# Second cross-attention of a decoder: turned copies behind the exponentials, products ahead of turning

## What is computed

```python
scores = jnp.einsum('bhqd,bhkd->bhqk', qh, kh) / math.sqrt(D_K)
scores = jnp.where(mask == 0, -jnp.inf, scores)
attn = jax.nn.softmax(scores, axis=-1)
attn = jnp.nan_to_num(attn, nan=0.0)
x = jnp.einsum('bhqk,bhkd->bhqd', attn, vh)
```

## Time and profile before

| what | value |
|---|---|
| median of 3 runs | 1338.29 us (1337.8 to 1340.01) |
| span of the profiled execution | 1336.9 us |
| busy PE / DVE / ACT / POOL | 86% / 82% / 62% / 61% |
| second attention, first scores to last scores | 1055.1 to 1261.0 us |
| rows of the profile that the change touches | L1088 to L1097 (DVE), L872 and L882 (ACT), L977 (POOL), L708 and L637 (PE) |

### The profile page before, as it was taken

The page is one execution under the profiler, slowest core; times in us unless marked ns, Lnnn a source line. Parts: engine busy times, 40 slices in busy tenths (PEclk is TensorE's granted clock), DMA queues, the critical chain, the costliest instruction groups (busy, mean ns, idle before and its releaser), DMA issues.

```text
span 1336.9 us, 17670 instructions
## 1 busy us (share of the span) xinstructions
PE 1155.3 (86%) x6026; PEld 672.1 (50%) x6026; DVE 1095.1 (82%) x1618; ACT 828.6 (62%) x1827; POOL 821.0 (61%) x743
## 2 busy tenths in 40 slices
PE   7798888878588999989989899899987888888874
PEld 4555555544244544545545455455454555555544
DVE  3577777575889999999999999999999768776556
ACT  2555555565477677866777668776754365566564
POOL 6001111100698998988989989899899344455405
PEclk9899999988889999999999989999897999999975
DMA  6000002000602305015041060230500300100000
GB/s 203 13 12 13 12 12 71 1 1 5 226 8 94 147 1 198 17 48 193 1 169 45 1 241 1 94 120 1 198 31 0 80 17 17 32 17 2 1 1 25
DMA packets 22142, 79.15 MB, mean 59 GB/s; under 512 B 4935, under 2 KB 8847, under 8 KB 21138
## 3 DMA queue, kind: packets, MB, share of 16 engines
q1 hardware_dynamic: 22054, 78.02, 16.8%
HBM read 76.77 MB, written 1.24 MB: 58 GB/s over the span
## 4 chain that ended last, share of the span: by engine, by line
PE 38%; DVE 33%; POOL 10%; ACT 10%; issue 7%; DMA 0%; SPq 0%; ACTq 0%; DVEq 0%; POOLq 0%
PE ps L637 36%; DVE ps L1954 10%; POOL arena L1868 6%; DVE arena L1959 4%; DVE arena L1957 4%; DVE hstat L1097 4%; ACT arena L872 3%; POOL arena L1880 2%; ACT ps L1751 2%; PE ps L708 2%; DVE arena L1917 2%; ACT L632 1%; ACT arena L882 1%; DVE arena L1085 1%; DVE arena L1063 1%
## 5 line engine op out<-in xcount | busy, mean ns | idle before, releaser
L637 PE MATMUL ps<-arena 128*32 128x100 f32 (+8 forms) x3300 | 521.0, 383 | 81.7 <-ACT arena L872 26.1
L1868 POOL TENSOR_TENSOR arena<-arena 128x1600 f32<-128x1600 f32 x128 | 456.4, 3580 | 35.4 <-DVE ps L1954 27.2
L637 PEld LDWEIGHTS ps<-arena 128*32 128x32 f32 (+6 forms) x3300 | 262.3, 146 | 298.2 <-issue 109.2
L637 PE MATMUL ps<-arena,ident 128*128 128x400 f32 x1024 | 386.2, 528 | 29.3 <-POOL arena L1880 19.6
L1751 ACT ACTIVATE ps<-arena 128x400 f32<-128x400 f32 x512 | 282.9, 590 | 184.5 <-DVE arena L1957 151.3
L1954 DVE TENSOR_TENSOR_SCAN ps<-ps,arena 128x800 f32<-128x800 f32 x176 | 320.6, 1822 | 22.7 <-ACT ps L1751 17.0
L637 PEld LDWEIGHTS ps<-arena,ident 128*128 128x128 f32 x1024 | 201.9, 200 | 197.6 <-issue 29.2
L872 ACT ACTIVATE arena<-ps,hstat 100x361 f32<-100x361 f32 x256 | 143.6, 563 | 107.1 <-DVE hstat L1097 107.0
L610 POOL TENSOR_SCALAR stat<-stat 100x1 f32<-100x1 f32 (+1 forms) x44 | 8.6, 196 | 289.8 <-DVE stat L591 288.6
L1957 DVE TENSOR_TENSOR arena<-ps,arena 128x800 f32<-128x800 f32 x176 | 174.4, 991 | 6.0
L1097 DVE TENSOR_REDUCE hstat<-ps 100x2 f32<-100x722 f32 x128 | 115.7, 905 | 68.7 <-PE ps L637 68.2
(11 more groups left out here) (191 smaller groups left out, 1000.9 us busy)
## 6 DMA issues: line engine op xcount, KB each, us to landing
arena<-bc_scratch SPq DMA_DIRECT2D x64, 800.0 KB, 6.7
arena<-in_ctxT SPq DMA_DIRECT2D x16, 361.0 KB, 4.1
arena<-in_w_in SPq DMA_DIRECT2D x4, 1024.0 KB, 4.9
arena<-in_expT SPq DMA_DIRECT2D x1, 2048.0 KB, 12.6
arena<-in_w_out SPq DMA_DIRECT2D x4, 512.0 KB, 3.2
arena<-in_mask SPq DMA_DIRECT2D x8, 141.0 KB
arena<-in_xT SPq DMA_DIRECT2D x2, 400.0 KB, 3.9
x_tok<-in_x_tok SPq DMA_DIRECT2D x1, 800.0 KB
```

The costliest lines, as they stand in the source:

```text
L637: return nc.tensor.matmul(outp, lhsT, rhs, start=first, stop=last)
L1868: nc.gpsimd.tensor_tensor(bx[:, unit % BX].rearrange("p (j t) -> p j t", j=SEGMENT), bbc[:, nq].rearrange("p (j t) -> p j t", j=SEGMENT), ...
```

## The change

The second attention gets loops of its own, by whole groups. On PE a group is now scores, values of group n-2, all other products of the four steps, and then all three T of group n-1 together. ACT does the four exponentials of a group in a row, then the copies of K, XT, FT and of the attention output, and last the three copies of T. The mask products signal after the second and after the fourth head, so that the first maximum can begin after two. DVE takes one reciprocal of all four sums at the start of the next group, ahead of both maxima; the product with `anyv` is gone there, and POOL's scaling takes `anyv` as its second factor in place of the constant 1.0. The table of steps changes: K0 and K1 at steps 0 and 4, the values at 5, 10 and 12, XT at 9, Q at 14, O at 8, the second norm at 9 and 13, FT at 16, the peak and copy of the result at 17 (for the last batch O, norm, peak and FT stay at their old steps). Batch 1 no longer has steps of its own. `dve_mask` also waits for the scaling of older groups, since POOL now reads `anyv`.

```diff
 
 AT = {
     "K": (0, 1),
-    "K1": (6, 7),
     "V0": (2, 3, 4),
...
-    "V": ((8, 18, 19), (10, 13, 14)),
+    "V": (8, 18, 19),
     "Q": 9,
     "Qc": 9,
     "xo": 14,
...
     "N2": 17,
     "N2e": 20,
-    "1k": (3, 5),
...
+    "1k": (3, 4),
+    "1K": (0, 4),
+    "1V": (5, 10, 12),
+    "1m": 2,
+    "1x": 3,
     "1xe": 5,
-    "1XT": 7,
-    "1XTc": 7,
-    "1Q": 9,
-    "1Qc": 9,
-    "1O": 5,
-    "1N": 6,
-    "1Ne": 8,
-    "1A": 9,
-    "1FT": 11,
-    "1FTc": 11,
+    "1XT": 9,
+    "1Q": 14,
+    "1O": (8, 5),
+    "1N": (9, 6),
+    "1Ne": (13, 8),
+    "1A": (17, 9),
+    "1FT": (16, 11),
     "pO": 2,
     "aK": 2,
     "aQ": 4,
...
         STEPS = range(-H, H * (B + 1) + 6)
...
 
+        def ended(g, name):
+
+            yield from (b for b in fin(g, AT[name][0]) if b < B - 1)
+            yield from (b for b in fin(g, AT[name][1]) if b == B - 1)
+
         def keys_at(g, layer):
...
-                    if b != 1 or layer == 0:
+                if layer == 0:
+                    for b in pre(g, AT["K"][c]):
                         yield b, c
-                if layer == 1 and g == AT["K1"][c]:
-                    yield 1, c
+                    continue
+                for b in pre(g, AT["1K"][c]):
+                    if b > 0:
+                        yield b, c
 
...
+                    for b in pre(g, AT["1V"][kc]):
+                        yield b, kc
+                    continue
                 for b in pre(g, AT["V0"][kc]):
                     if b == 0:
                         yield b, kc
-                for b in pre(g, AT["V"][layer][kc]):
+                for b in pre(g, AT["V"][kc]):
                     if b > 0:
                         yield b, kc
+
+        def quad_steps(n):
+            return range(QUAD * n, QUAD * n + QUAD)
 
         def has_head(v):
             return 0 <= v < B * H
...
             for i in range(QUAD):
                 r = slice(32 * i, 32 * i + 32)
                 last = mm(ps[0:S, i, 0:SK], a.qm[r, par, qd], a.kT[r, par, qd // 2], True, a.layer == 0)
-            if a.layer == 1:
-                for i in range(QUAD):
-                    last = mm(ps[0:S, i, 0:SK], identb[0:S, 0:S], a.mb[0:S, par, 0:SK], False, True)
-            last.then_inc(a.s_full, 1)
+            if a.layer == 0:
+                last.then_inc(a.s_full, 1)
+                return
+            for i in range(QUAD):
+                last = mm(ps[0:S, i, 0:SK], identb[0:S, 0:S], a.mb[0:S, par, 0:SK], False, True)
+                if i % 2:
+                    last.then_inc(a.s_full, 1)
 
         def pe_probs(pe, a, n, r):
 
...
                 elif has_quad(n - 1):
                     pe_probs(pe, a, n - 1, i - 1)
                 for b, c in keys_at(g, a.layer):
                     pe_k(pe, a, b, b % 2, c)
-                for b, kc in values_at(g, a.layer):
...
+        def pe_attn_last(pe, a):
+            for n in LAST_QUADS:
+                if has_quad(n):
+                    pe_scores(pe, a, n)
+                if n < 2:
+                    pm_out(pe, ROUNDS - 1, n)
+                if has_quad(n - 2):
+                    pe_values(pe, a, n - 2)
+                for g in quad_steps(n):
+                    for b, c in keys_at(g, 1):
+                        pe_k(pe, a, b, b % 2, c)
+                    for b, kc in values_at(g, 1):
+                        pe_v(pe, a, b, b % 2, kc)
...
-                    for b in fin(g, AT["1O"]):
+                    for b in ended(g, "1O"):
...
-                    for b in fin(g, AT["1FT"]):
+                    for b in ended(g, "1FT"):
...
+                if has_quad(n - 1):
+                    for r in range(KC):
+                        pe_probs(pe, a, n - 1, r)
...
-                wait(act, a.s_full, (b - 1) * QUADS)
+                wait(act, a.s_full, (b - 1) * QUADS * (a.layer + 1))
...
+        def act_attn_last(act, a):
+            for n in LAST_QUADS:
+                for g in quad_steps(n):
+                    if has_head(g):
+                        act_exp(act, a, g)
+                for g in quad_steps(n):
+                    for b in fin(g, AT["C"]):
+                        act.wait_ge(a.av_full, (b + 1) * QUADS)
+                        w = QUADS // a.share * S
+                        nc.scalar.activation(a.cT[:, b % 2, 0:w], ps[:, 4, 0:w], ACT.Copy).then_inc(a.cT_ready, 1)
...
-                    for b in pre(g, AT["1XTc"]):
+                    for b, c in keys_at(g, 1):
+                        act_k(act, a, b, b % 2, c)
+                    for b in pre(g, AT["1XT"]):
...
-                    for b in fin(g, AT["1FTc"]):
+                    for b in ended(g, "1FT"):
...
+                if has_quad(n - 1):
+                    for r in range(KC):
+                        act_probs(act, a, n - 1, r)
...
-        def pool_scale(pool, a, n, i, k):
-
-            pool.wait_ge(a.rs_ready, 2 * n + i // 2 + 1)
-            for j in range(i, i + k):
+        def pool_scale(pool, a, n):
+
+            pool.wait_ge(a.rs_ready, n + 1)
+            bp = n // QUADS % 2
+            for j in range(QUAD):
                 e = a.es[0:S, (n * QUAD + j) % 8, 0:SK]
                 rs = hstat[0:S, n % 2, 2, j:j + 1]
                 ready = a.prob_ready[j // 2]
-                nc.gpsimd.tensor_scalar(e, e, rs, 1.0, ALU.mult, ALU.mult).then_inc(ready, 1)
+                nc.gpsimd.tensor_scalar(e, e, rs, anyv[0:S, bp:bp + 1], ALU.mult, ALU.mult).then_inc(ready, 1)
...
                 if a.layer == 1 and i == 0 and has_quad(n - 1):
-                    pool_scale(pool, a, n - 1, 2, 2)
-                if a.layer == 1 and i == 2 and has_quad(n):
-                    pool_scale(pool, a, n, 0, 2)
+                    pool_scale(pool, a, n - 1)
...
             dve.wait_ge(a.exp_ready, n * QUAD + i + k)
...
-            if a.layer == 0:
-
-                step(nc.vector.reciprocal(st[:, 2, i:i + k], st[:, 1, i:i + k]))
-                for j in range(i, i + k):
-                    e = a.es[0:S, (n * QUAD + j) % 8, 0:SK]
-                    nc.vector.tensor_scalar(e, e, st[:, 2, j:j + 1], CLIP_EPS, ALU.mult,
-                                            ALU.max).then_inc(a.prob_ready[j // 2], 1)
-            else:
-                step(nc.vector.reciprocal(st[:, 3, i:i + k], st[:, 1, i:i + k]))
-
-                bp = n // QUADS % 2
-                nc.vector.tensor_scalar(st[:, 2, i:i + k], st[:, 3, i:i + k], anyv[0:S, bp:bp + 1], None,
-                                        ALU.mult).then_inc(a.rs_ready, 1)
+            step(nc.vector.reciprocal(st[:, 2, i:i + k], st[:, 1, i:i + k]))
+            for j in range(i, i + k):
+                e = a.es[0:S, (n * QUAD + j) % 8, 0:SK]
+                nc.vector.tensor_scalar(e, e, st[:, 2, j:j + 1], CLIP_EPS, ALU.mult,
+                                        ALU.max).then_inc(a.prob_ready[j // 2], 1)
+
+        def dve_sums_last(dve, a, n):
+
+            dve.wait_ge(a.exp_ready, n * QUAD + QUAD)
+            st = hstat[0:S, n % 2]
+            nc.vector.reciprocal(st[:, 2, 0:QUAD], st[:, 1, 0:QUAD]).then_inc(a.rs_ready, 1)
 
         def dve_max(dve, a, n, i):
 
-            dve.wait_ge(a.s_full, n + 1)
+            dve.wait_ge(a.s_full, n + 1 if a.layer == 0 else 2 * n + i // 2 + 1)
             nc.vector.tensor_reduce(hstat[0:S, n % 2, 0, i:i + 2], ps[0:S, i:i + 2, 0:SK], AX.X, ALU.max,
                                     negate=True).then_inc(a.max_ready, 1)
 
...
+            if has_quad(n - 1):
+                dve_sums_last(dve, a, n - 1)
+            if has_quad(n):
+                dve_max(dve, a, n, 0)
+                dve_max(dve, a, n, 2)
 
         def dve_sums(dve, a, b):
 
...
             for g in steps:
-                dve_quad(dve, a, g)
+                if a.layer == 0:
+                    dve_quad(dve, a, g)
+                elif g % QUAD == 0:
+                    dve_quad_last(dve, a, g // QUAD)
                 if a.layer == 1:
-                    for b in pre(g, 2):
+                    for b in pre(g, AT["1m"]):
                         dve_mask(dve, a, b, b % 2)
...
 
             dve.wait_ge(a.ctx_in[par], 16 * b + 16 * (2 - par))
             v = a.vm[0:S, par]
+            if b >= 2:
+                for ready in a.prob_ready:
+                    dve.wait_ge(ready, 2 * QUADS * (b - 1))
             vstep.mark(nc.vector.tensor_scalar(v, a.mk[0:S, par], 0.0, None, ALU.is_equal))
             vstep.settle()
             vstep.mark(nc.vector.tensor_reduce(anyv[0:S, 2 + par:3 + par], v, AX.X, ALU.min))
```

97 lines of the change are left out of this document (51 added, 46 removed).

## The result

The changed kernel takes **1314.89 us** (1314.17 to 1320.03, 4 runs), where the kernel before takes 1338.05 (1334.85 to 1340.01, 4 runs). The ratio is 0.983, with an interval from 0.980 to 0.986.

What follows compares the result with a forecast made beforehand. PE was taken as near its limit, with waits in a 5.86 us loop of PE, DVE and ACT. Gains 12.3 + 0 + 1.5 = 13.8 us off 1336.9 give 1323.1, plus 1.4 for the median: 1324.5 us, range 1316 to 1336.

Steps and rivals of the forecast that it cites:

- Part 1, the ring: Scores, maximum, exponentials across PE, DVE, ACT: first maximum at 1.25 us instead of 1.65, next scores at 4.5 instead of 5.8.
- Part 2, PE: PE's own work and bank waits set most group lengths; a batch without quantising takes 23.55 us, against 25.3.
- Part 3, quantising: DVE's quantising still delays the next group's maximum; with it, groups 4 to 31 take 165.0 against 177.3, gaining 12.3 us.
- q1 grows by 1.9 to about 8.2: A batch's second group lengthens because DVE, quantising from the first, is free 3.1 us after scores; maximum due at 1.25.
- q3, which grows by 0.7: A batch's fourth group lengthens to 6.35 us because DVE's quantising from the third ends 2.2 us into it.
- The peak and copy, 0.7: DVE in a batch's first group: the result's peak and copy, moved there, take 0.7 us after the second maximum.
- the mask and query rows, 2.65: DVE in a batch's first group: mask and query rows take 2.65 us, ending at 6.35.
- the piece, 2.7 to 2.9: Quantising on DVE at the end of a batch's first group takes 2.7 to 2.9 us, ending at 9.1.
- Part 4, POOL and the reciprocals: Two-pointer scaling on POOL takes 0.67 us, 2.7 a group with 4 to 5 available; fewer DVE reciprocals count nothing extra.
- Part 5, the two ends: Start after the scanning stage gains 0 (-1 to +1); the last groups and final turnings gain 1.5 us (0 to 3).
- The slower one: Rival: POOL becomes the bound if two-pointer scaling takes 1.6 us, deciding from about 1.3; 1363 us, chance 0.17.
- More: Rival: the clock stays up and DVE's pieces overlap better, gain 19 us, 1319 us; PE floor 22.1 a batch; chance 0.07.

Runs made afterwards that it cites:

- the moved pieces: The changed kernel, but the quantising pieces that stood at the end of each batch's first group stand at the end of its second: 1313.2 us.
- the filler: The changed kernel with eight more POOL operations, into a buffer nobody reads, in the first group of every batch from the first on: 1320.28 us.
- halves: The changed kernel, but DVE takes reciprocals two at a time, each with an anyv product, and POOL scales two heads at a time with one pointer: 1331.39 us.
- with two signals: The kernel before with one part of the change alone, the masks signalling after two and after four products: 1334.88 us.
- the kernel with turnings first: The changed kernel, but from group 5 the previous group's turnings precede other products on PE, their copies other copies on ACT: 1373.43 us, then 1370.8.

## Why the prediction was wrong, by its own steps

**Part 1, the ring: right.** The first maximum comes at 1.34 us (1.25 forecast), exponentials stand 0.55 apart, and where PE has little else, the next scores come after 4.62 (4.5). The second signal gives 0.3 us in a group, save in q1 with quantising, where DVE is late anyway, and in q3 of batches 4 to 6.

**Part 2, PE: right in its way, off in q3.** q0, q1, q2 are 5.92, 6.14, 5.69 for 5.95, 6.25, 5.7; PE waits for K's copy by 0.89 in q0, as named. q3 is 5.32 for 5.65: DVE frees Q0 and Q1 sooner (its two operations end 4.7 us into the group), so no T waits for them. Over six batches that is 2.0 us of the miss, and the smaller amounts of q0 to q2 are 0.9.

**Part 3, quantising: the failed step.** Forecast were 9.15 us of growth over batches 1 to 5, and 4.6 came. "q1 grows by 1.9 to about 8.2" was 1.2 to 7.33, and "q3, which grows by 0.7" was 0 to 0.2: in batch 3 DVE was free 1.6 us into q3, not 2.2, and a maximum that comes 0.3 late is hidden there behind PE's products. The method stood: DVE's end in q0, less the time at which the maximum is due, is q1's growth, and the moved pieces show that nothing else is in it. The terms were too long: DVE was to reach q1's maximum 9.1 us into q0, and does so at 8.5. The peak and copy, 0.7, take 0.52; the mask and query rows, 2.65, take 2.41; the piece, 2.7 to 2.9, takes 2.56. This has two causes.

The first is POOL. The last mask operation and the four first ones of the piece at 1104.56 were read with POOL scaling beside DVE. In the changed kernel POOL scales four heads at the head of a group and then rests, and they take 0.34 for 0.51 and 1.11 for 1.53. With the filler on POOL the peak, copy, mask and query rows take 3.5 us, where they take 2.93.

The second is the way of adding. The durations of the peak and the copy were summed, but one starts before the other's record ends, and the query rows were counted up to the end of their last row, where the next operation starts 0.1 us sooner. POOL had no part in the 0.7. It was idle beside these two rows in the kernel before too, where the next operation starts 0.53 us behind the peak's start at 1158.38:

```profile
1158.71 0.28 DVE L1243 COPY x_tok<-arena 100x256 f32<-100x256 f32 x1
1158.91 0.15 DVE L1088 RECIPROCAL hstat<-hstat 100x2 f32<-100x2 f32 x1
...
1159.42 1.14 POOL L977 TENSOR_SCALAR arena<-arena,hstat 100x361 f32<-100x361 f32 x2 [1.77 <-DVE hstat L1091]
```

Of the 0.42 us that these two terms were too long, 0.17 is the mask operation beside POOL and the other 0.25 the adding. That the filler brings them to 3.5, near the 3.35 of the forecast, is chance: it makes longer what was not longer in the kernel before.

**Part 4, POOL and the reciprocals.** "0.67" for the scaling was 0.654. (The prediction also calls the old form's cost "the value taken here"; that is 0.573, and it took 0.67.) "DVE waits there anyway, so I count nothing" fell: halves in the changed kernel cost 13.6 us by the trace, with the clock's part in it. "POOL needs 2.7 us a group and has 4 to 5" fell as well, since 1.6 us more in a group were not free, though it did no harm here.

**Part 5, the two ends.** Behind the scanning stage, group 4 comes 31.6 us after those last matmuls. In the kernel before it is 33.5 in the first trace and 32.1 in the second, as those matmuls ran at the lower clock once (4.36 us for 2.95), and 31.5 with two signals. The changed kernel's second trace has 33.0, at the lower clock again. So the order gives nothing there, as counted, and the signal 0.6. "Fuller groups may hold full clock" did not hold as put: it fell in group 29 behind a wait of 1.58 us and cost batch 7 1.0 us (it is 14.6 in five other traces of this order, with the clock up). For the last stretch, 1.5 us forecast, nothing can be told from its whole length. Its head tells more: the last twelve turnings start 8.50 and 7.36 us behind the last scores in the two traces of the kernel before, 6.78 and 6.77 in the changed one, and 6.55 in the old order with two signals. So with the scores at full clock the end gives 0.6 us at most, and the two signals alone give no less. The last scaling ends 7.5 us behind the scores, where 7.0 were forecast.

**The sum.** From 4 to 31, 12.3 forecast and 18.7 found: 4.5 of the difference is Part 3, 2.9 Part 2, and batch 7 gave back 1.1. How the other 4.5 of the 23.2 us between the medians divide between the ends and the scanning stage's scatter stays open.

**The rivals.** The slower one was priced at 1363 us for 1.6 us a scaling and "from about 1.3". It takes 1363.5 at 1.31, and 1.6 us more a group, 1.06 a scaling, already cost 14.5 us from 4 to 31. Its point lies lower, as POOL's work is in a chain (norm's root, scaling, T), not a sum over a batch. "More", 1319 us with a floor of 22.1 us of PE a batch, was the nearest and got 0.07. Its gain of 19 us is what came, but its floor does not bound it: seven batches of 22.1 are 154.7, 22.6 less than 177.3, and PE's busy time fell to 21.6 a batch.

## What to carry to other kernels

Put work that is ready ahead of work that waits for a helper engine: undoing this for the turnings and their copies cost 51 us, more than undoing any other part of the change. When an order changes, take again every duration of DVE if POOL's work moves beside it. Add durations from start to start and not as they stand in the rows: here this alone was 0.25 us a batch. And sum a helper engine's time along its chain in one group, with what it waits for, before calling it free.

## What was not expected of the hardware

- A wait of PE of 2.4 us cost 1.5 us more behind it, since the granted clock fell to 1.2 GHz; waits of 1.4 to 1.7 us mostly didn't, and sometimes did: behind 1.58 us ahead of group 29, and behind 1.60 us ahead of q2 of batch 2 in the changed kernel's second trace, where the first trace has the same wait and kept 2.4 GHz. So the length of one wait doesn't decide it. In the kernel with turnings first the lower clock cost some 17 us by the estimate above.
- POOL's scaling with two pointers takes 0.65 us for 361 columns and with one pointer 0.57; with subtract and multiply it takes 1.59. The Trainium skill (GPSIMD Engine Reference, 4.1 Engine selection) calls one input roughly line-rate; both pairs have one input here, and the mixed pair takes 2.4 times as long as the like one.
- An operation of POOL on a single column takes 0.19 us alone (0.55 the one of L633) and 0.65 to 0.69 beside DVE's operations of 0.69 us. The other way, DVE's copy of a row takes 0.28 us alone and 1.96 beside a run of POOL's operations.
